# Splitting the query and key projections without the vector engine, in a cross-attention kernel on one Trainium2 core

## The reference

```python
q = _heads(hidden_states @ to_q_w)
h_txt = _sdpa(q, _heads(ehs_txt @ to_k_w), _heads(ehs_txt @ to_v_w))
h_obj = _sdpa(q, _heads(ehs_obj @ to_k_object_w), _heads(ehs_obj @ to_v_object_w))
h_oth = _sdpa(q, _heads(ehs_oth @ to_k_others_w), _heads(ehs_oth @ to_v_others_w))
h_ip = _sdpa(q, _heads(ehs_ip @ to_k_ip_w), _heads(ehs_ip @ to_v_ip_w))
out = _merge(h_txt) + _merge(h_obj) + _merge(h_oth) + _merge(h_ip)
out = out @ to_out_w + to_out_b + residual
```

## Time and profile before

| | |
|---|---|
| time, median of three runs | 1705.54 us (1705.48 to 1706.51) |
| the profiled execution's own time | 1707.59 us |
| its span in the trace | 1705.5 us |
| mean granted clock of PE | 0.992 of full speed |
| length of one turn of the loop in the trace | 49.8 us |
| DMA traffic | 366 MB, mean 215 GB/s |

### The profile page before, as it was taken

How to read it: one execution, slowest core, us unless ns; L and a number is a source line. 1 busy time by engine, 2 the same in 40 slices (tenths; PEclk the granted TensorE clock), 3 DMA queues, 4 the chain that set the end, 5 groups by cost and what they waited for, 6 DMA issues and landing times.

```text
span 1705.5 us, 49968 instructions
## 1 busy us (share of the span) xinstructions
PE 1623.6 (95%) x15632; PEld 1377.6 (81%) x15632; DVE 1498.3 (88%) x3537; ACT 1076.2 (63%) x1989; POOL 1342.3 (79%) x1581
## 2 busy tenths in 40 slices
PE   6959999999999999999999999999999999999976
PEld 3658888888888888888888888888888888888865
DVE  4249999999999999999999999999999999999996
ACT  1126666666666666676666667666666666666664
POOL 4248888888888888888888888888888888888765
PEclk9979999999999999999999999999999999999999
DMA  8579889888988988898898889889888988988851
GB/s 303 140 208 234 205 228 239 203 227 217 241 206 227 237 205 227 217 238 209 227 235 205 227 218 238 208 230 232 207 226 219 238 208 231 230 207 229 207 124 32
DMA packets 423236, 366.24 MB, mean 215 GB/s; under 512 B 19041, under 2 KB 394274, under 8 KB 418850
## 3 DMA queue, kind: packets, MB, share of 16 engines
q1 hardware_dynamic: 423202, 365.80, 84.7%
HBM read 216.38 MB, written 149.34 MB: 214 GB/s over the span
## 4 chain that ended last, share of the span: by engine, by line
PE 71%; DVE 17%; issue 7%; POOL 2%; SPq 1%; DMA 1%; DVEq 1%; ACT 0%; POOLq 0%
PE job_ps L837 24%; PE ring_ps L913 13%; PE ring_ps L926 7%; PE ring_ps L936 7%; PE s_ps L886 6%; PE job_ps L863 5%; DVE l_seg L718 5%; DVE probs L691 5%; DVE m_seg L675 3%; PE job_ps L856 2%; PE ring_ps L804 2%; PE job_ps L866 2%; DVE rest L708 1%; POOL probs L491 1%; PE job_ps L874 1%
## 5 line engine op out<-in xcount | busy, mean ns | idle before, releaser
L491 POOL TENSOR_TENSOR probs<-probs,rl 128x616 f32<-128x616 f32 (+1 forms) x640 | 630.1, 1007 | 237.2 <-DVE rl L729 236.8
L837 PE MATMUL job_ps<-c_in,w_kv 128*128 128x172 f32 (+1 forms) x2560 | 575.5, 368 | 22.4 <-DVE rest L708 22.4
L592 ACT ACTIVATE pT<-ring_ps 128x512 f32<-128x512 f32 x640 | 378.6, 599 | 313.1 <-PE ring_ps L913 309.1
L837 PEld LDWEIGHTS job_ps<-c_in,w_kv 128*128 128x128 f32 x2560 | 421.4, 190 | 101.0 <-DVE rest L708 30.0
L718 DVE TENSOR_REDUCE l_seg<-probs 128x8 f32<-128x616 f32 (+1 forms) x640 | 385.4, 644 | 23.0 <-ACT probs L580 23.0
L913 PE MATMUL ring_ps<-ident,probs 128*128 128x128 f32 x2560 | 389.9, 277 | 10.1 <-DVE y_all L740 8.5
L691 DVE TENSOR_TENSOR probs<-s_ps,m_seg 128x616 f32<-128x616 f32 (+1 forms) x640 | 387.8, 648 | 0.0
L675 DVE TENSOR_REDUCE m_seg<-s_ps 128x8 f32<-128x616 f32 (+1 forms) x640 | 371.6, 623 | 3.5 <-issue 0.2
L580 ACT ACTIVATE probs<-probs 128x1024 f32<-128x1024 f32 x320 | 337.6, 1055 | 33.2 <-DVE probs L695 33.1
L913 PEld LDWEIGHTS ring_ps<-ident,probs 128*128 128x128 f32 x2560 | 290.0, 143 | 66.7 <-issue 25.1
L472 POOL TENSOR_TENSOR parts<-rest,zero 128x512 bf16<-128x512 f32 (+1 forms) x192 | 186.2, 970 | 50.7 <-DVE rest L708 50.7
(11 more groups left out here) (54 smaller groups left out, 1598.2 us busy)
## 6 DMA issues: line engine op xcount, KB each, us to landing
q_all<-q_scratch SPq DMA_DIRECT2D x64, 960.0 KB, 8.1
k_all<-k_scratch SPq DMA_DIRECT2D x64, 960.0 KB, 12.3
c_in<-in_cT SPq DMA_DIRECT2D x32, 1024.0 KB, 5.1
x_raw<-in_xT SPq DMA_DIRECT2D x32, 768.0 KB, 4.8
q_scratch<-parts SPq DMA_DIRECT2D x64, 384.0 KB, 3.0
k_scratch<-parts SPq DMA_DIRECT2D x64, 384.0 KB, 5.2
x_res<-in_x SPq DMA_DIRECT2D x128, 160.0 KB, 3.8
out<-y_all SPq DMA_DIRECT2D x128, 160.0 KB, 3.5
```

What stands on the lines that cost most here:

```text
L491: pool.tensor_tensor(pr[:, :, a:e], pr[:, :, a:e], r[:, :, s:s + 1].broadcast_to((P, OH, e - a)), ALU.mult)
L592: act.activation(pT[:, h:h + QH, :], ring_ps[i][:, :].rearrange("p (h s) -> p h s", h=QH), ACT.Copy)\
L837: last = pe.matmul(dst[:, :, a:e], w_kv[:, l, k, i * P:(i + 1) * P], c_in[:, k, :, a:e], start=(k == 0), stop=(k == CK - 1))
```

## The change

In the loop, DVE no longer takes part in a split. ACT copies the job from PSUM twice: whole, in fp32, to `whole` (the buffer that was `rest`), then rounded to bf16 as before; `part1_made` now frees the bank. POOL subtracts in place (`make_rest`), a slot later ACT rounds that to the second part (`round_second`), and POOL subtracts again (`make_third`). In POOL's slot n, after `scale`, `make_third` comes for jobs that ended in slot n-2 (first place) or n-3 (second place), then `make_rest` for those of n-1 or n-2. The early jobs keep the old way. The store of the small tokens of groups 2 to 31 moves up in SP's queue, from behind the three query stores of group 1 to ahead of `load_c(1)`.

```diff
@@ SP, ahead of the loop
             load_small(1)
+            sp.dma_start(small_scr[2:G].rearrange("g p n -> p g n"), ...).then_inc(small_rest_stored, 16)
             load_c(1)
             for n in range(3):
                 store_parts(1, n)
-            sp.dma_start(small_scr[2:G].rearrange("g p n -> p g n"), ...).then_inc(small_rest_stored, 16)
             load_pair(0, 0, 1)
@@ POOL
+            def make_rest(g, n):
+                src = whole[0:r, n % 2, 0:w]
+                pool.wait_ge(part1_made, g * NSP + n + 1)
+                pool.tensor_tensor(src, src, parts[0:r, n % PR, 0, 0:w], ALU.subtract).then_inc(rest_made, 1)
+            def make_third(g, n):
+                pool.wait_ge(part2_made, (g - 2) * NSP + n + 1)
+                pool.tensor_tensor(parts[0:r, n % PR, 2, 0:w], whole[0:r, n % 2, 0:w], parts[0:r, n % PR, 1, 0:w],
+                                   ALU.subtract).then_inc(part3_made, 1)
@@ POOL slot
                 for at in range(2):
-                    for turn, job in ended(g, n - 2, at):
+                    for turn, job in ended(g, n - 2 - at, at):
                         if job in SPLITS:
-                            split(turn + 2, SPLITS.index(job))
+                            make_third(turn + 2, SPLITS.index(job))
+                for at in range(2):
+                    for turn, job in ended(g, n - 1 - at, at):
+                        if job in SPLITS:
+                            make_rest(turn + 2, SPLITS.index(job))
@@ ACT evacuate
+                    if not (isinstance(turn, int) and turn < 0):
+                        after(act, part3_made, g * NSP + m - 1)
+                        act.activation(whole[0:r, m % 2, 0:w], ps[0:r, 0:w], ACT.Copy)
                     after(act, parts_stored[m % PR], stored_count(g, m))
                     act.activation(parts[0:r, m % PR, 0, 0:w], ps[0:r, 0:w], ACT.Copy).then_inc(part1_made, 1)
+            def round_second(g, m):
+                act.wait_ge(rest_made, (g - 2) * NSP + m + 1)
+                act.activation(parts[0:r, m % PR, 1, 0:w], whole[0:r, m % 2, 0:w], ACT.Copy).then_inc(part2_made, 1)
@@ ACT slot, behind exponent and the first evacuations
+                for at in range(2):
+                    for turn, job in ended(g, n - 2 - at, at):
+                        if job in SPLITS:
+                            round_second(turn + 2, SPLITS.index(job))
@@ DVE slot
-                for at in range(2):
-                    for turn, job in ended(g, n - 1, at):
-                        if job in SPLITS:
-                            subtract_part(turn, job)
@@ PE wait_bank
-                    if other in SPLITS:
-                        pe.wait_ge(part_freed, split_count(g, other))
+                    if other in SPLITS and isinstance(t, int) and t < 0:
+                        pe.wait_ge(early_rest_made, split_count(g, other))
+                    elif other in SPLITS:
+                        pe.wait_ge(part1_made, split_count(g, other))
```

More of the change, by code:

```diff
@@ L182, in xattn_kernel @@
         parts = sb("parts", [P, PR, 3, NB * S], bf16)
-        rest = sb("rest", [P, 2, NB * S])
+        whole = sb("whole", [P, 2, NB * S])
         q_all = sb("q_all", [P, NPAIR * H * 2 * S], bf16)
@@ L234, in xattn_kernel @@
         job_filled = sem("job_filled")
-        part_freed = sem("part_freed")
+        early_rest_made = sem("early_rest_made")
+        early_second_made = sem("early_second_made")
         copy_freed = sem("copy_freed")
         part1_made = sem("part1_made")
+        rest_made = sem("rest_made")
         part2_made = sem("part2_made")
@@ L402, in _ @@
             load_small(1)
+            sp.dma_start(small_scr[2:G].rearrange("g p n -> p g n"),
+                         small_all[:, 2:G, :, :, :].rearrange("p g m b t -> p g (m b t)")).then_inc(small_rest_stored, 16)
             load_c(1)
@@ L405, in _ @@
                 store_parts(1, n)
-            sp.dma_start(small_scr[2:G].rearrange("g p n -> p g n"),
-                         small_all[:, 2:G, :, :, :].rearrange("p g m b t -> p g (m b t)")).then_inc(small_rest_stored, 16)
             load_pair(0, 0, 1)
@@ L462, in _, with split_early @@
                                pattern=[[-1, P]], channel_multiplier=1).then_inc(ident_made, 1)
-            def split(g, n):
+            def split_early(g, n):
                 r, w = split_shape(n)
-                src, dst = rest[0:r, n % 2, 0:w], parts[0:r, n % PR, :, 0:w]
-                pool.wait_ge(part_freed, g * NSP + n + 1)
+                src, dst = whole[0:r, n % 2, 0:w], parts[0:r, n % PR, :, 0:w]
+                pool.wait_ge(early_rest_made, g * NSP + n + 1)
                 after(pool, parts_stored[n % PR], stored_count(g, n))
                 pool.tensor_tensor(dst[:, 1, :], src, zero[0:r, :].broadcast_to((r, w)), ALU.add)\
-                    .then_inc(part2_made, 1)
-                pool.wait_ge(part2_made, g * NSP + n + 1)
+                    .then_inc(early_second_made, 1)
+                pool.wait_ge(early_second_made, g * NSP + n + 1)
                 pool.tensor_tensor(dst[:, 2, :], src, dst[:, 1, :], ALU.subtract).then_inc(part3_made, 1)
+            def make_rest(g, n):
+                r, w = split_shape(n)
+                src = whole[0:r, n % 2, 0:w]
+                pool.wait_ge(part1_made, g * NSP + n + 1)
+                pool.tensor_tensor(src, src, parts[0:r, n % PR, 0, 0:w], ALU.subtract).then_inc(rest_made, 1)
+            def make_third(g, n):
+                r, w = split_shape(n)
+                pool.wait_ge(part2_made, (g - 2) * NSP + n + 1)
+                pool.tensor_tensor(parts[0:r, n % PR, 2, 0:w], whole[0:r, n % 2, 0:w], parts[0:r, n % PR, 1, 0:w],
+                                   ALU.subtract).then_inc(part3_made, 1)
             def x_low(g, k):
@@ L506, in _ @@
             for n in range(3):
-                split(0, n)
+                split_early(0, n)
             for k in range(CX):
@@ L510, in _ @@
             for n in range(3, NSP):
-                split(0, n)
+                split_early(0, n)
             for n in range(NSP):
-                split(1, n)
+                split_early(1, n)
             for k in range(CX):
@@ L566, in evacuate @@
                            .then_inc(v_head_copied, 1)
+            def round_second(g, m):
+                r, w = split_shape(m)
+                act.wait_ge(rest_made, (g - 2) * NSP + m + 1)
+                act.activation(parts[0:r, m % PR, 1, 0:w], whole[0:r, m % 2, 0:w], ACT.Copy).then_inc(part2_made, 1)
             def x_high(g, k):
@@ L707, in subtract_part @@
                 after(dve, part3_made, g * NSP + m - 1)
-                dve.tensor_tensor(rest[0:r, m % 2, 0:w], ps[0:r, 0:w], parts[0:r, m % PR, 0, 0:w], ALU.subtract)\
-                   .then_inc(part_freed, 1)
+                dve.tensor_tensor(whole[0:r, m % 2, 0:w], ps[0:r, 0:w], parts[0:r, m % PR, 0, 0:w], ALU.subtract)\
+                   .then_inc(early_rest_made, 1)
             def sum_up(g, o):
```

## The result

The changed kernel takes 1687.32 us (median of four runs, 1686.33 to 1689.03) against 1705.61: a ratio of 0.989, with a 95% interval of 0.9878 to 0.9902. It is 18.3 us faster; 1690 was predicted. The profiled execution took 1687.23 us, with a span of 1685.5. The span is 20.0 us shorter than that of before, mainly because the profiled execution of before lay 2.0 us above its median.

A forecast was written before the change was run, and what follows sets the result against it. PE sets the loop's pace, other engines counting only where it waits. Gains of 7.8 (kv0's bank), 1 (q0's) and 7 (store) sum to 15.8 us, giving 1689.7, said as 1690; range 1678 to 1709, likeliest 1683 to 1696.

The forecast's parts named there:

- signs of being wrong: PE waiting for L494 (now L510) or `k_all`, ACT waiting for POOL ahead of its copies, or a turn not below 49.8.
- The bank of kv0: Slot 8, where kv1 wants it: ACT frees it 0.26 us sooner per turn, 7.8 us in 30 turns; 0.44 us wait remains.
- The bank of q0: Wanted by q1: a first-turn wait of 1.14 us goes, taken as 1 us once; nothing in later turns.
- nothing else holds it: Steady loop: PE's only waits are 30 of 0.70 us ahead of L837, released by DVE's L708.
- ceiling of 21 us: The loop: the most a freer DVE can give, 0.70 us per turn.
- The store: Ahead of the loop: moving the small-token store lands `x_raw` of group 2 sooner, 7 us; bounds 8 and 0.
- The slip by `c_in`: Ahead of the loop: `c_in` of group 1 lands near 87.7, PE waits some 3 us, hidden in its later stop.
- even share: Ahead of the loop: if store and `c_in` shared the DMA engines evenly, `c_in` lands near 82, nothing slips, same sum.
- The costs of nothing: Added ACT work, POOL's order, ACT's wait for POOL, and late third parts in the loop: each judged to cost 0.
- POOL's string: From `oT_low` in slot 0 to `scale` of octet 1: ends at 823.95, 0.8 us ahead of PE's transposes; cost 0.
- the slower rival: POOL's work in slots 9 to 2 binds: 2 us late would give 1726; chance 0.18.
- the two bounds: POOL's in-place subtraction, which had no row: between 1161 and 1277 ns, taken as 1.2 us.

The follow-up runs named there:

- dve_refilled: The changed kernel with a DVE reduction of 512 columns, read by nobody, wherever DVE's subtraction was: 1688.95 us, 0.9896.
- kv0_twice: The changed kernel with one more ACT copy of kv0 (0.48 us, result unused) ahead of the rounded one: 1703.40 us, 0.9987 to the kernel before.
- q0_half_subtracted: The kernel before with DVE's subtraction of q0 in the loop over half the columns only: 1701.64 us, 0.9968.
- kv0_first_q0_stored_first: The changed kernel with ACT evacuating kv0 ahead of slot 7's second transposes copy, and q0's store earlier in SP's queue: 1666.31 us, 0.9763 to the kernel before.
- c_in_first: The changed kernel with the small-token store behind the load of c_in of group 1, not ahead of it: 1691.31 us, 0.9912 to the kernel before.

## Why the prediction was right

**The bound.** PE set the pace and was held only for banks. dve_refilled and kv0_twice show it from two sides: DVE's load is worth 0.04 us per turn, 0.48 us of ACT work ahead of kv0's release is worth 0.49. All of PE's listed waits from 150 us on are for that bank; there are none for L510 or `k_all`, and ACT's own list has no wait for POOL, so none of the signs of being wrong came in the loop.

**The bank of kv0.** Predicted: release by the rounded copy, 0.26 us sooner, 0.44 of the wait left. Measured: 0.25 sooner, 0.45 left. 7.5 us in 30 turns for 7.8.

**The bank of q0.** This term was mis-sized. It was taken as 1 us once and as nothing in the loop, because the list of waits had no row for it. It was 0.15 us in each turn, 4.5 us in 30, as q0_half_subtracted shows. The failing step is the reading "nothing else holds it": the rows of before had DVE's subtraction of q0 ending 0.06 us ahead of q1 in the loop too. For the same reason the ceiling of 21 us was wrong: kv0's wait costs 0.86 + 0.10 us per turn, q0's 0.15, together 1.11 x 30 = 33 us; kv0_first_q0_stored_first has taken nearly all of it in the loop (49.80 to 48.7).

**The store.** Predicted 7 us, all by `x_raw`; it gave 6.0. The lead at the first turn's kv1 is 7.3 us, which has q1's first wait and kv0's 0.25 in it. The slip by `c_in` was mis-sized too. Its load landed 13.5 us after its issue, at 88.6, near the 87.7 reckoned behind the store and far from the 82 of an even share; PE waited 4.87 us for it, for 3. Then the early kv0 took 5.17 us in place of 3.51, at a mean granted clock of 0.67 from 88.73 to 93.90. So the early jobs slipped by 6.0 us (112.04 for 106.03), and their end came at 114.33 where the prediction had 111. PE's stop shrank by 12.0 us, not 10. The slip was still hidden, but with 1.4 us to spare, and that was in part luck.

**The costs of nothing.** The copy of transposes in slot 8 ended at 837.93, PE wanted it at 838.46: 0.53 to spare for 0.5. POOL's string, beside the earlier trace rows:

```profile
801.07 1.00 POOL L539 TENSOR_TENSOR oT<-oT_raw,oT 128x384 fp32r<-128x384 f32 x1 [1.64 <-ACT oT L635]
...
810.84 0.32 POOL L510 TENSOR_TENSOR probs<-probs,rl 128x64 f32<-128x64 f32 x1
...
830.71 1.16 POOL L490 TENSOR_TENSOR parts<-whole,parts 128x512 bf16<-128x512 f32 x1
```

From `oT_low` at 801.07 to the end of `scale` of octet 1 it took 10.1 us (10.25 predicted) and ended 1.06 us ahead of PE's transposes at 812.22, so the slower rival had no hold. `make_third` of q1 ended at 831.87, 2.9 us ahead of the whole copy. The in-place subtraction, unseen before, takes 1164 ns at 128x512, close to the lower of the two bounds (1161). The prediction's estimate of 1.11 us was 0.05 us short. `k_all` was issued at 817.61 and landed 13.3 us later, 3.5 us ahead of the scores at 834.42. Only q0's store was nearer than thought, and in the changed kernel it cost 0.1 us in one turn: there ACT's rounded copy of kv0 starts at 588.33, 0.59 us behind the whole copy in place of 0.48, and the store landed at 588.31.

**The sum.** Predicted 7.8 + 1 + 7 = 15.8. In the traces it is 7.3 up to kv1 of the first turn, 11.8 in the next 29 turns (7.3 by kv0's bank, 4.4 by q0's, 0.1 rounding) and 0.9 behind (the last kv1 started at 1595.87 before and 1576.73 after, 19.1 apart, the ends are 20.0 apart). The medians differ by 18.3. That 1690 came within 3 us of 1687.32 is a right mechanism with some luck in the number: in the traces the loop gave 11.8 us where 7.8 were predicted, the start and the first turn 7.3 where it was 8, and of the 20.0 us 1.7 are left out of the medians, since the profiled execution of before was a long one.

## What to carry to other kernels

Where one engine sets the pace, an edit is worth what it changes at the instruction that this engine waits for; 0.5 us of ACT work cost the turn its whole length at kv0 and nothing at kv1 and kv2. Measure a wait from start to start against the same pair of groups elsewhere, not by the idle column: here 0.70 us listed were 0.96, and a wait of 0.15 us in each turn was not listed. When a producer is moved later, follow its buffer as well as its result: who overwrites it next, and what stands ahead of its store in the queue.

## What the runs showed that was not expected

A PE group that starts after such a wait also runs longer: kv1's first half takes 2.18 us to the next group with a wait of 0.45, 0.70 or 0.94 us ahead of it, and 2.08 without; why was not tried. An SP issue behind large loads was blocked for 5.63 us, and the urgent store behind it was late by that much. And a stop of PE of 1.42 us was followed by a granted clock of 1.00, one of 4.35 us by 0.50. The length of the stop does not decide alone: after 2.66 us the next eight score matmuls took 1.03 us at 0.50 in the changed kernel (106.10) and 0.62 us at 1.00 in c_in_first (104.18), where the clock was 0.65 in the group behind them.
